# Mixture-of-experts stage: the first expert's bias of odd groups moves from TensorE to ScalarE

## What is computed

```python
gate_scores = softmax(einsum('btd,ed->bte', x, Wg))
topk_val, topk_idx = top_k(gate_scores, 2)          # two experts for a token
topk_val = topk_val / (topk_val.sum(-1, keepdims=True) + 1e-9)
for e in range(8):
    h = einsum('btd,hd->bth', x, W1[e]) + b1[e]     # 128 -> 512, b1 is the bias of this change
    a, b = split(h, 2, axis=-1)                     # 256 and 256
    eo = einsum('bth,dh->btd', a * sigmoid(b), Wo) + bo
    out = out + eo * comb[..., e:e + 1]             # comb: the two shares of a token
x = x + gb * out
```

## Time and profile before

| | us |
|---|---|
| time, median of 3 runs | 733.64 |
| lowest and highest run | 732.01, 734.11 |
| span of the profiled execution | 731.3 |
| the expert stage in it, from the first bias product to the last copy L2009 | 490.0 to 717.0 |

### The profile page before, as it was taken

The page is one execution under the profiler, slowest core; times in us unless marked ns, Lnnn a source line. Parts: engine busy times, 40 slices in busy tenths (PEclk is TensorE's granted clock), DMA queues, the critical chain, the costliest instruction groups (busy, mean ns, idle before and its releaser), DMA issues. The chain is left out here.

```text
span 731.3 us, 14263 instructions
## 1 busy us (share of the span) xinstructions
PE 618.6 (85%) x3515; PEld 471.0 (64%) x3515; DVE 602.0 (82%) x1384; ACT 523.2 (72%) x1321; POOL 538.1 (74%) x657
## 2 busy tenths in 40 slices
PE   2656889999999899978888877557599999999994
PEld 0433566767777667756555675426488888888884
DVE  6389989999999999987999745655478888888884
ACT  3656668899888877886675676625377888888883
POOL 5467657899999779899869876553756666666666
PEclk8799989999999999999999899758989999999998
DMA  3999888889988889878889799343345444444530
GB/s 108 258 142 134 112 112 132 135 153 144 156 137 154 140 127 133 161 147 154 146 155 162 181 315 297 134 126 90 89 76 85 77 78 78 82 81 82 85 69 1
DMA packets 103300, 95.58 MB, mean 131 GB/s; under 512 B 14523, under 2 KB 82710, under 8 KB 102966
## 3 DMA queue, kind: packets, MB, share of 16 engines
q1 hardware_dynamic: 85846, 79.69, 58.1%
q0 software_dynamic: 16176, 12.75, 9.8%
q10 hardware_dynamic: 1200, 2.23, 0.8%
HBM read 35.47 MB, written 25.61 MB: 84 GB/s over the span
## 5 line engine op out<-in xcount | busy, mean ns | idle before, releaser
L2065 POOL DMA_INDIRECT out<-res,index x91 | 141.7, 1557 | 76.8 <-DVE res L2146 59.4
L843 POOL TENSOR_TENSOR rs_prod<-rT,state_rows 128x512 f32<-128x512 f32 x128 | 139.4, 1096 | 44.2 <-DVE state_rows L1528 42.8
L1281 PEld LDWEIGHTS ps_k<-w,gel 128*128 128x128 f32 x512 | 61.6, 200 | 15.9 <-issue 12.2
L1989 ACT ACTIVATE sig<-ps_a 128x256 f32<-128x256 f32 x91 | 35.1, 385 | 49.0 <-issue 18.6
L1281 PE MATMUL ps_k<-w,gel 128*128 128x128 f32 x512 | 64.2, 286 | 2.4 <-ACT gel L1098 2.4
L2113 DVE SCALAR_TENSOR_TENSOR half<-ps_b,xg,sig 128x256 f32<-128x256 f32 x91 | 43.6, 479 | 26.5 <-ACT sig L1993 24.3
L1246 PE MATMUL ps_f<-hnT_hi,mix_hi 128*128 128x512 f32 x128 | 54.5, 426 | 8.9 <-DVE hnT_lo L1651 7.7
L2106 DVE SCALAR_TENSOR_TENSOR ps_a<-ps_a,xg,sig 128x256 f32<-128x256 f32 x91 | 44.4, 487 | 17.8 <-ACT sig L1989 9.2
L1943 PEld LDWEIGHTS ps_y<-out_w,gT 128*128 128x128 f32 x364 | 49.0, 197 | 9.8 <-ACT gT L2022 5.4
L1943 PE MATMUL ps_y<-out_w,gT 128*128 128x128 f32 x364 | 50.2, 282 | 4.7 <-ACT gT L2022 3.4
L2015 ACT ACTIVATE ps_b<-bias_rows 128x512 f32 x89 | 53.0, 595 | 0.0
(11 more groups left out here) (357 smaller groups left out, 2000.6 us busy)
## 6 DMA issues: line engine op xcount, KB each, us to landing
v_spread<-vT SPq DMA_DIRECT2D x128, 256.0 KB, 5.2
xg<-sorted_scratch SPq DMA_DIRECT2D x91, 130.0 KB
xin<-in_L_attn_x SPq DMA_DIRECT2D x16, 256.0 KB, 6.5
x<-in_L_attn_x SPq DMA_DIRECT2D x16, 256.0 KB
out<-x SPq DMA_DIRECT2D x16, 256.0 KB
sorted_scratch<-gel SPq DMA_DIRECT2D x4, 910.0 KB, 8.3
tokens_scratch<-h SPq DMA_DIRECT2D x12, 256.0 KB
raw_w<-in_L_ffn_W ACTq DMA_DIRECT2D x2, 1024.0 KB, 9.3
```

What stands on the lines that cost most here:

```text
L843: pool.tensor_tensor(rs_prod[:, p, idx % 4], rT[p][:], state[idx][:, p * NT:(p + 1) * NT], ALU.mult).then_inc(s["rs_ready"], 1)
L1281: mm = pe.matmul(ps_k2[:, q * P:(q + 1) * P], gel[c][:, q * P:(q + 1) * P], w2[:, c, :], start=(c == 0), stop=(c == NF - 1))
L2065: pool.indirect_dma_start(out_rows, bass.IndirectOffsetOnAxis(ap=index[k % RESULTS][:, i:i + 1], axis=0), res[k % RESULTS][:, i, :], None, ...
```

## The change

From group 3 on, ScalarE also copies the first expert's bias of odd groups, in front of the copy of the second expert's bias. TensorE issues no bias product from the second pair on and waits for that copy instead. 44 products L1898 go (odd groups 3 to 89) and 44 copies L2009 come. The copy for group `2k+1` waits for the `join` of group `2k-1`, by the same rule as for even groups.

```diff
@@ TensorE, group(k, i)
-                if j < FIRST_SEED or i == 1:
+                if j < FIRST_SEED:
                     bias(ps_a[j % 2], low)
                 else:
-                    pe.wait_ge(s["low_seeded"], k - FIRST_SEED // 2 + 1)
+                    pe.wait_ge(s["low_seeded"], j - FIRST_SEED + 1)
@@ ScalarE, experts_of(j)
-                low = (both & (PACK - 1)).with_bounds(min_val=0, max_val=(E - 1) * H2) if j % 2 == 0 else None
+                low = (both & (PACK - 1)).with_bounds(min_val=0, max_val=(E - 1) * H2)
@@ ScalarE, the loop over k
             for k in range(PAIRS):
                 low, high = experts_of(2 * k + 1)
                 low_gate(2 * k)
+                low_seed(2 * k + 1, low)
                 seed(2 * k + 1, high)
                 high_gate(2 * k)
```

## The result

| | before | changed |
|---|---|---|
| first comparison, median (runs) | 732.83 us (4) | 746.04 us (4) |
| ratio, 95% interval | | 1.0181 [1.0149, 1.0212] |
| second comparison, median (runs) | 732.56 us (22) | 747.46 us (6) |
| ratio, 95% interval | | 1.0203 [1.0168, 1.0238] |

The change makes the kernel slower, by 13.2 us in the first comparison and 14.9 us in the second. The forecast was 749.0 us, 15.4 above the kernel before, with a range of 742 to 757.

A forecast was written before the change was run, and what follows sets the result against it. A 4.62 us loop through ScalarE and VectorE, not TensorE, was taken as the bound. 39 periods each 0.38 longer, 14.8 us, plus 0.6 for the start make 15.4 us, so 749.0 us, range 742 to 757.

The forecast's parts named there:

- the loop: ScalarE and VectorE steps from one even group's join to the next, without TensorE: 4.62 us, the whole period before the change.
- The rival with TensorE as the bound: TensorE's work sets the regular stretch's period; removing 0.23 us in each of 44 pairs gives 723.5 us; chance 0.08.
- The price of the copy: On ScalarE ahead of the copy of ps_b1: 0.54 us less slack of 0.16 makes each period 0.38 us longer.
- 0.16 of slack: Before VectorE's high_half: the sigmoid of ps_b0 could let it start at 604.64, but it starts at 604.80.
- The new waits: ScalarE's copy waits for a join, 0.09 us to spare; TensorE waits for the copy, 0.15 us, covered; neither costs anything.
- the uneven start of the stage: Five pairs before 536 us, with ScalarE mostly idle: a loss of 0 to 2.7 us, taken as 0.6.
- No effect: Rival: the copy falls into ScalarE's idle 0.87 us, the period stays 4.62, so 733.6 us; chance 0.05.
- a smaller loss by a shorter way through an idle TensorE: Rival: copy's end to sigmoid of ps_a0 shortens by 0.10 us or twice that; 741 to 745 us; chance 0.06.
- The heavier loss: Rival: TensorE's idle share grows to 12%, its clock falls in some pairs; three pairs would give 759 us; chance 0.07.

The follow-up runs named there:

- e1: Kernel before with the 44 bias products of odd groups from 3 on left out and nothing in their place: ratio 0.9991, 733.16 us.
- e7: Kernel before with VectorE reordered (join ahead of rest_pair, finish behind the next low_half) and the 44 bias products left out: ratio 0.9842, 720.30 us.
- e6: Kernel before with only VectorE reordered (join ahead of rest_pair, finish of the pair before behind the next low_half): ratio 0.9973, 730.15 us.
- e3: Kernel before plus 43 spare ScalarE copies nobody waits for, behind the sigmoid of ps_a0, ahead of the copy of ps_b1: ratio 1.0233, 750.48 us.
- e4: Kernel before plus the same 43 spare ScalarE copies, behind a pair's last copy and ahead of the next sigmoid of ps_a0: ratio 0.9985, 733.27 us.

## Why the prediction was right

The direction and the size held, and the loop is the step that carried them.

**The bound.** That TensorE's 40.00 of 40 us did not bind is shown by e1: 44 products less, no time less. That the loop did is shown by e7, where the same products are out and the loop is shorter: 4.35 instead of 4.63. e6 adds that the two limits were close. The rival with TensorE as the bound had 723.5 us here, and the measurement decides against it. The rule of the Trainium skill ("Perfetto Trace Analysis", section "Identifying the Most-Contended Engine"), to optimize the engine with the highest occupancy first, spoke for this rival; this trace does not bear it out, since less work on that engine gave nothing until the chain was shorter.

**The price of the copy.** 0.54 less 0.16 of slack, 0.38 a pair, came as 5.01 - 4.63 = 0.38. Of the parts, the copy ahead of another copy holds it up by 0.52 (609.75 to 610.27) and not 0.54. On the other side, from copy to sigmoid 0.52, from sigmoid to `high_half` 0.41, from there to `rest_pair` 0.40, and from products to sigmoid 1.00 are each within 0.01 of the rows before. So the term for the copy was 0.02 too large, and three others were 0.01 too small; that the sum comes out within 0.01 is in part luck. The estimate from the Trainium skill, "ScalarE: Activation LUTs", section "What ACT_TABLE_LOAD costs", 0.52 us, agrees with this row better than my 0.54 did.

**The new waits.** The copy's wait for the join leaves no idle time, and TensorE's wait for the copy is there (610.69, 0.34 behind the copy's end). Neither costs anything, as forecast: e3 has the loss without them.

**The term that was off.** For the uneven start of the stage I took 0.6 us of loss. From the first copy L2009 to the last one the kernel before takes 717.0 - 495.2 = 221.8 us. The changed kernel takes 727.5 - 493.9 = 233.6 in the first profile and 732.0 - 495.8 = 236.2 in the second, 11.8 and 14.4 more, by these rows, first profile first:

```profile
L2009 ACT ACTIVATE ps_a<-bias_rows x89: 596/598/602, 493.9 to 727.5; 128x512 f32 x89
```

```profile
L2009 ACT ACTIVATE ps_a<-bias_rows x89: 595/598/602, 495.8 to 732.0; 128x512 f32 x89
```

With 39 x 0.38 = 14.8 from the regular part, the start gave 3.0 and 0.4 us back. The start shows no loss, and one execution differs from the next there by more than my term: of the same changed kernel, by 2.6 us. The granted clock differs with it. From 480 to 520 us it is 0.86 in the first profile and 0.78 in the second, against 0.75 before:

```profile
480.00:520.00 40.00, 29.88 (x119) 19.85 (x119) 23.02 (x75) 19.26 (x44) 21.58 (x22) 0.86 0.42 117
```

```profile
480.00:520.00 40.00, 28.80 (x108) 19.68 (x109) 24.05 (x78) 17.95 (x43) 22.15 (x21) 0.78 0.40 114
```

The execution with the higher clock gave back more. Whether some of it is due to the change is open; two profiles don't tell. With this the loss of the first comparison, 13.2 us, lies at the low end of the forecast's own 12.8 to 21.1, and its 746.04 us just below that range's 746.4, inside the stated 742 to 757.

**The rivals.** No effect, a TensorE bound, and a smaller loss by a shorter way through an idle TensorE are all ruled out by the period of 5.01. The heavier loss did not come either: the clock stays at 2.4 GHz in the regular window although TensorE waits in every pair.

## What to carry to other kernels

Before moving work from a "busy" engine to an "idle" one, write down the loop that returns to the same instruction one period later, start to start, across all engines. If the steps add up to the period, only what is on that loop counts, up to the next longest one (here 0.05 us a pair away): an instruction taken off another engine is worth nothing, and one put in front of a step of the loop costs its length less the slack at that place, whatever the idle share of its engine. Then look for the place in the stream where the idle time lies: here the same copy cost 0.39 us a pair behind the even group's sigmoid (e3) and nothing ahead of it (e4).

## What the runs showed of the hardware

An idle share says little about where work fits. ScalarE at 36.58 of 40 us ran without loss (e4), and with 32.92 of 40 us it carried a copy whose place cost 15 us. TensorE is shown busy for 39.86 of 40 us in e1 although it has less work than before in the same time. A product's row lasts past the moment at which the next one starts: the expert products follow each other by 0.23 us and are shown with 0.39, and L1943's row before the change ends 0.20 us behind the start of the next product. So a wait of that length is nearly hidden: in e1, 0.03 of 0.23 us shows.
